# First cross attention: two heads scored in fp32 from the context, q stack turned on the chip, keys split in folded blocks, biases added on VectorE

## The reference

```python
q = heads(layernorm(x)); k = v = heads(ctx_1024)           # no projection here
u = einsum('hbqd,hbkd->hbqk', q, k) * scale / sqrt(16)
logits = tanh(u) * exp(log_C)
attn = softmax(where(mask, -inf, logits))
x = x + (attn @ v) @ W_out.T
```

## Time and profile before

| | us |
|---|---|
| median of 3 runs | 863.05 |
| lowest and highest | 860.47, 866.04 |
| profiled execution: span | 865.0 |
| TensorE busy in the span | 682.0 (79%) |
| ScalarE busy | 469.3 (54%) |
| VectorE busy | 432.3 (50%) |
| first cross attention, first score to last exp | 56.04 to 328.16 |

### The profile page before, as it was taken

The page is one execution under the profiler, slowest core; times in us unless marked ns, Lnnn a source line. Parts: engine busy times, 40 slices in busy tenths (PEclk is TensorE's granted clock), DMA queues, the critical chain, the costliest instruction groups (busy, mean ns, idle before and its releaser), DMA issues. The chain is left out here.

```text
span 865.0 us, 14147 instructions
## 1 busy us (share of the span) xinstructions
PE 682.0 (79%) x4916; PEld 375.2 (43%) x4916; DVE 432.3 (50%) x962; ACT 469.3 (54%) x554; POOL 64.0 (7%) x87
## 2 busy tenths in 40 slices
PE   0029789999999996495418999999999879957798
PEld 0013335544544543374203444444444456745686
DVE  6505422222232223765618887878778333644544
ACT  1236669999999995272003666656666605603010
POOL 6010001010010100000200000000000110000000
PEclk9999879999999998699556999999999969988799
DMA  7579843333333211000376222222221090000000
GB/s 231 137 211 296 221 134 106 100 106 92 117 100 102 89 36 49 0 1 1 85 145 199 69 68 68 66 68 68 66 74 58 18 311 1 2 1 0 1 1 12
DMA packets 55767, 75.93 MB, mean 88 GB/s; under 512 B 8756, under 2 KB 40886, under 8 KB 55734
## 3 DMA queue, kind: packets, MB, share of 16 engines
q1 hardware_dynamic: 50642, 72.87, 28.8%
q10 hardware_dynamic: 5092, 2.63, 1.2%
HBM read 61.06 MB, written 13.63 MB: 86 GB/s over the span
## 5 line engine op out<-in xcount | busy, mean ns | idle before, releaser
L1282 DVE TENSOR_REDUCE sb_m_blk<-ps 128x1 f32<-128x512 f32 x256 | 166.8, 687 | 56.0 <-PE ps L1180 55.4
L1143 ACT ACTIVATE sb_probs<-ps 128x1024 f32<-128x1024 f32 x128 | 129.4, 1023 | 62.4 <-PE ps L1207 62.0
L546 ACT ACTIVATE sb_probs<-ps 128x1024 f32<-128x1024 f32 x128 | 124.3, 1017 | 52.2 <-PE ps L571 49.2
L548 ACT ACTIVATE sb_probs<-sb_probs,sb_neg_cap,sb_cap 128x4096 f32<-128x4096 f32 x32 | 121.6, 3801 | 1.1
L1180 PE MATMUL ps<-sb_k_st,sb_q_m 96*128 96x512 bf16 x256 | 98.2, 405 | 27.3 <-issue 20.6
L571 PE MATMUL ps<-sb_q_st,sb_k_st 115*128 115x256 bf16 x512 | 77.9, 289 | 41.3 <-DMA sb_k_st<-k_parts_l 41.0
L1207 PE MATMUL ps<-sb_q_st,sb_k_st 115*128 115x256 bf16 x512 | 78.2, 275 | 9.7 <-ACT sb_q_st L1152 9.0
L571 PEld LDWEIGHTS ps<-sb_q_st,sb_k_st 115*128 115x128 bf16 x512 | 44.3, 102 | 94.2 <-issue 62.1
L584 PE MATMUL ps<-sb_probs,sb_v_st 128*32 128x256 f32 x1024 | 78.2, 403 | 3.8 <-ACT sb_probs L548 3.6
L1224 PE MATMUL ps<-sb_probs,sb_v_st 128*32 128x256 f32 x1024 | 78.5, 390 | 1.8
L1207 PEld LDWEIGHTS ps<-sb_q_st,sb_k_st 115*128 115x128 bf16 x512 | 48.8, 101 | 30.6 <-issue 11.8
(11 more groups left out here) (232 smaller groups left out, 867.9 us busy)
## 6 DMA issues: line engine op xcount, KB each, us to landing
sb_k_st<-k_parts_l SPq DMA_DIRECT2D x192, 128.0 KB, 2.7
k_parts_l<-sb_v_proj SPq DMA_DIRECT2D x24, 256.0 KB
k_parts_l<-sb_early SPq DMA_DIRECT2D x48, 128.0 KB
sb_k_st<-k_parts_l SPq DMA_DIRECT2D x64, 64.0 KB, 2.5
sb_early<-ctxT SPq DMA_DIRECT2D x8, 512.0 KB, 3.7
sb_probs<-ctxT SPq DMA_DIRECT2D x4, 512.0 KB, 7.5
sb_v_rows<-ctx ACTq DMA_DIRECT2D x1, 2048.0 KB, 16.4
sb_v_proj<-ctxT SPq DMA_DIRECT2D x4, 512.0 KB, 6.8
```

The lines of the kernel that those rows point to most:

```text
L546: a.activation(probs[:, j % 2, 4 * g:4 * g + 4, :], scores_bank(g), ACT.Tanh).then_inc(s["tanh"], 1)
L548: a.activation(probs[:, j % 2], probs[:, j % 2], ACT.Exp, bias=k.neg_cap[:, 0:1], scale=k.cap[:, 0:1]).then_inc(s["exp"], 1)
L1143: nc.scalar.activation(probs[:, g], scores_bank(g), ACT.Exp).then_inc(s["exp"], 1)
L1282: v.tensor_reduce(k.m_blk[:, q, blk:blk + 1], k.ps[:, 6 + idx % 2, :], AX.X, ALU.max).then_inc(s["m_read"], 1)
```

## The change

stage_prepare is gone and its work is inside stage_cross0. Heads 0 and 1 (the first four units) are scored in fp32: their channels of the transposed context are loaded straight into 16-row slabs at partitions 0, 32, 64 and 96 (`load_first_keys`), and each score group is four fp32 matmuls of 16 rows, two on each of two slabs (`qk_first`). The q stack is built from rows on VectorE (`split_rows`) and turned by 32 TensorE transposes (`turn`) instead of through DRAM. Both use the space of `k_st` until the loads for iteration 1. The split keys start at head 2, in seven blocks of 128 partitions x 1024 keys, where the first three fold two or four ranges of keys of the same heads onto the partitions. `kd0` is now laid out part, channel, key, and a unit's keys are read from it as 2 parts x 16 channels x 2048 keys for 32 destination rows. VectorE splits block 0 ahead of the first accumulator copy, and blocks 1 to 6 between the end of its first iteration and its second. The biases of the layer 1 projection are added on VectorE when the result is read, and the bias matmuls are gone. The early weights are loaded behind iteration 1, the context rows come in halves of keys on SyncE, and TensorE waits once for all expert weights.

```diff
-    k.kd0 = nc.dram_tensor("k_parts_l0", [H, PARTS * DH, S2], BF16, kind="Internal").ap()
+    k.kd0 = nc.dram_tensor("k_parts_l0", [PARTS, D, S2], BF16, kind="Internal").ap()
...
+    k.q_rows = k.k_st[:, 0:2, :]...
+    k.k_first = k.k_st[:, 2:4, :]...
...
-def store_k_parts(k, sp, n, parts):
...
+def load_first_keys(k, sp, e, units, done):
+
+    for r in range(2):
+        rows = slice(64 * e + 32 * r, 64 * e + 32 * r + DH)
+        src = k.i["ctxT"][e * DH:(e + 1) * DH, :].rearrange("d (u g r n) -> r d u g n", u=2, g=GROUPS, r=2)[r]
+        for u in units:
+            sp.dma_start(k.k_first[rows, u], src[:, u]).then_inc(done, 16)
+
+BLOCKS = [(2, 4, 0), (4, 2, 0), (4, 2, 1)] + [(8, 1, n) for n in range(SPLITS)]
...
+def store_block(k, sp, n, parts):
+
+    h0, folds, _ = BLOCKS[n]
+    rows = P // folds
+    sp.wait_ge(k.sem("k0_split"), n + 1)
+    for a in range(folds):
+        sp.dma_start(k.kd0.rearrange("s r n -> r s n")[h0 * DH:h0 * DH + rows, :, block_keys(n, a)],
+                     parts[a * rows:(a + 1) * rows, n % 2]).then_inc(k.sem(f"k0_stored{n % 2}"), 16)
...
+def load_k0_unit(k, sp, h, half, slot, loaded):
+
+    ks = slice(half * UNIT_KEYS, (half + 1) * UNIT_KEYS)
+    kd = k.kd0.rearrange("s (h d) n -> s h d n", d=DH)
+    for r in range(PARTS):
+        sp.dma_start(k.k_st[2 * DH * r:2 * DH * (r + 1), slot, :], kd[0:2, h, :, ks]).then_inc(loaded, 16)
+    sp.dma_start(k.k_st[LOROW:STACK, slot, :], kd[2, h, :, ks]).then_inc(loaded, 16)
...
-def stage_prepare(k):
...
@@ SP of stage_cross0
+            load_first_keys(k, sp, 0, [0], first_in[0])
+            load_ctx_rows(k, sp, 0)
+            load_first_keys(k, sp, 0, [1], first_in[1])
+            load_first_keys(k, sp, 1, [0, 1], first_in[2])
+            load_ctx_rows(k, sp, 1)
+            load_block(k, sp, 0, blk)
...
+            store_block(k, sp, 0, parts)
+            load_block(k, sp, 3, blk)
+            sp.wait_ge(k.sem("k0_stored0"), blocks_stored(0))
+            sp.wait_ge(s["q_turned"], H // 4)
+            for j in range(2):
+                load_keys(0, j)
+            for j in range(2):
+                store_kd1(0, j)
+            sp.wait_ge(s["scores"], 16)
+            for j in range(2, 4):
+                load_keys(0, j)
+            next_ctx(0)
+            for n in range(1, len(BLOCKS)):
+                store_block(k, sp, n, parts)
+                if 3 < n + 3 < len(BLOCKS):
+                    load_block(k, sp, n + 3, blk)
+            for n in (len(BLOCKS) - 2, len(BLOCKS) - 1):
+                sp.wait_ge(k.sem(f"k0_stored{n % 2}"), blocks_stored(n))
+            body(1, True)
+            load_early_weights(k, sp)
...
@@ POOL
-            link(g.memset(k.k_st[MAXROW:LOROW, :, :], 1.0))
-            link(g.memset(k.q_all[MAXROW:LOROW, :, :], 0.0))
...
@@ PE
+            def qk_first(j, g):
...
+                for c in range(2):
+                    for r in range(2):
+                        rows = slice(64 * e + 32 * r, 64 * e + 32 * r + DH)
+                        last = t.matmul(out[:, 2 * r + c, :], k.k_first[rows, u, g, c * P:(c + 1) * P], k.q_first[rows, :],
+                                        start=True, stop=True)
...
+            def turn(n):
...
+                        last = t.transpose(turned(n)[:, (h * QT + q) * P:(h * QT + q + 1) * P],
+                                           k.q_rows[:, q, 4 * n + h, :], k.ident_bf[:, :])
...
-                    last = t.matmul(o, k.bkv1[0:1, 0, j * P:(j + 1) * P], k.ones_row[0:1, 0:CBLK], start=False, stop=True)
...
-                        last = t.matmul(o, k.ones_row[0:1, 0:P], k.bkv1[0:1, 1, :], start=False, stop=True)
...
@@ DVE
-                v.tensor_copy(k.kd_bf[:, j, 0, :], src).then_inc(s["kd_ops"], 1)
+                v.tensor_scalar(k.kd_bf[:, j, 0, :], src, bias, None, ALU.add).then_inc(s["kd_ops"], 1)
...
+            split_rows(k, link, k.xn[:, :, :], k.q_rows).then_inc(s["q_rows"], 1)
+            for n in range(H // 4):
+                dve.wait_ge(s["q_turned"], n + 1)
+                v.tensor_copy(k.q_all[0:STACK, 4 * n:4 * n + 4, :].rearrange("p h q -> p (h q)"), turned(n)).then_inc(s["q_stack"], 1)
+            v.memset(k.k_st[MAXROW:LOROW, 0:2, :], 1.0).then_inc(s["k_ones"], 1)
+            split_block(0)
+            copy_acc(0, 0)
+            split_k(0, 0, True)
+            split_k(0, 1, True)
+            normalise(0, 0)
...
+            v_rows(0, 2)
+            v_rows(0, 3)
+            for n in range(1, len(BLOCKS)):
+                split_block(n)
+            body(1)
...
@@ last stage
-                pe.wait_ge(k.sem(f"f_exp_in{n}"), 48)
+                if n == 0:
+                    pe.wait_ge(k.sem("f_exp_in"), 16 * 3 * (N_EXP + 1))
```

More of the change, by code:

```diff
@@ L245, in layer_norm @@
     rsqrt(k, link, QT)
+def layer_norm(k, dve, link, src, dst, done):
+    v = k.nc.vector
+    norm_stats(k, link, src)
     for t in range(QT):
@@ L346, in load_early_weights @@
                      i["L0_attn_w_projT"].rearrange("(g m d) n -> m d g n", m=4, d=DH)[m]).then_inc(w2, 16)
-def stage_prepare(k):
[L351 to L384, removed]
-            link(g.memset(k.k_st[MAXROW:LOROW, :, :], 1.0))
-            link(g.memset(k.q_all[MAXROW:LOROW, :, :], 0.0))
[L389 to L440, removed]
-            dve.wait_ge(k.sem("pool_order"), 6)
-            for b in range(2):
-                link(v.tensor_copy(k.v_st[:, b, :, DH], k.keep[:, :]))
-        @block.tensor
-        def _(pe):
-            pe.wait_ge(k.sem("pool_order"), 2)
-            pe.wait_ge(k.sem("xn0"), QT)
-            transpose_rows(k, k.xn, 0, k.sem("xnT_ps"))
@@ L579, in pv @@
                     pe.wait_ge(s["exp"], 4 * it + j + 1)
-                    if j % 2 == 0 and not first:
+                    if first:
+                        if j == 0:
+                            pe.wait_ge(s["keep"], 3)
+                        pe.wait_ge(s["v_half"], (1, 3, 3, 4)[j])
+                    elif j % 2 == 0:
                         pe.wait_ge(s["o_read"], 2 * it + b - 1)
@@ L626, in body @@
                             if not (first and j == 0):
-                                pv(pit, pj, c, first)
+                                pv(pit, pj, c, fresh if j == 0 else first)
+                        if first and j == 1 and g == 0:
+                            turn(0)
+                            turn(1)
+                    if j == 1 and first:
+                        turn(2)
+                        turn(3)
                     if j == 1 and not first:
@@ L631, in body @@
                         sel(2 * it, 0)
-                    project(it, j, first)
-            pe.wait_ge(k.sem("w1_in"), 64)
+                    if not first:
+                        project(it, j, False)
+                    elif j >= 2:
+                        project(0, 2 * (j - 2), True)
+                        project(0, 2 * (j - 2) + 1, True)
+            pe.wait_ge(k.sem("pool_order"), 2)
+            pe.wait_ge(s["xq"], QT)
+            for q in range(QT):
+                last = t.transpose(k.ps[:, 7, q * P:(q + 1) * P], k.xq[:, q, :], k.ident[:, :])
+            last.then_inc(s["xqT"], 1)
             body(0, True)
-            with pe.Fori(1, H // 2) as it:
+            body(1, False, True)
+            with pe.Fori(2, H // 2) as it:
                 body(it, False)
@@ L712, in _ @@
+            for n in (len(BLOCKS) - 2, len(BLOCKS) - 1):
+                dve.wait_ge(k.sem(f"k0_stored{n % 2}"), blocks_stored(n))
+            with dve.Fori(2, H // 2) as it:
+                body(it)
             copy_acc(H - 1, 1)
```

273 lines of the change are left out of this document (187 added, 86 removed).

## The result

| | before | after |
|---|---|---|
| median (runs) | 864.54 (4) | 934.16 (4) |
| lowest to highest | 860.47 to 866.08 | 933.66 to 934.57 |
| ratio, 95% interval | | 1.081, 1.077 to 1.084 |
| profiled span | 865.0 | 932.9 |
| mean TensorE clock, share of 2.4 GHz | 0.919 | 0.864 |

The first score comes 45 us earlier, the last exp 63 us later, and the rest of the program loses 5 us more. ScalarE's timeline of the kernel after (start, length, line, tiles, count, and in brackets the idle time ahead with what ended it) shows both; it answers to the earlier trace rows.

A forecast was written before the change was run, and what follows sets the result against it. ScalarE bounds the first cross attention before, the two-engine key-load queue after. Stretches to 144.2, weights' iteration to 188.0, four iterations of 40.5 to 350.0, end 380.6: 52.4 us later, span 917.4, median 916, range 888 to 970.

The forecast's parts named there:

- The head: Start of the first cross attention: first scores at about 10.7 instead of 56.04, 45 us earlier.
- rival 3: First four units: fp32 units take twice as long, so the earlier start gives nothing; 12 us more, no separate chance.
- Two engines: Key loads read as 2x16x2048 are carried by two DMA engines: 7.87 us a unit, and the queue becomes the bound.
- The period: Steady cross attention iteration: 40.5 us, bounds 36.7 and 41.3, against 30.7 on ScalarE.
- gaps in the queue of 1 to 2 us at three places: Per iteration, the late context block and slow TensorE clock delay key loads, leaving the DMA queue empty.
- The sum: Cross attention's terms added up: stage end at 380.6 against 328.16, 52.4 later; span 917.4, median 916.
- then the keys of units 8 to 11 and a context block: 144.2: After the last block store lands at 107.5, the queue loads these until 144.2.
- The bound from below: Whole kernel on two engines with no gaps and a start 4 us better: 895.
- rival 2: Key loads on two slower engines, 19.1 GB/s each: iterations about 50 us, 121 later, 984; chance 0.16.
- Priced at nothing: Removed bias matmuls (22.2 + 19.8 us of TensorE), VectorE's sums and the one expert-weight wait: no effect on time.
- Rival 1: Key loads use all 16 engines after all: stage ends at 286.7, 41.5 earlier, 822; chance 0.12.
- key loads landing 10 us and more: Sign in the changed trace for two engines: key loads land this long after issue instead of 2.7.

The follow-up runs named there:

- e3: The kernel before with only the new kd0 layout, its 128x1024 stores and 2x16x2048 key loads: 969.64, ratio 1.121.
- e1: The changed kernel with each 32-row key load issued as two of 16 rows, seven transfers a unit instead of four: 842.41, ratio 0.973.
- e2: The changed kernel with stack rows ordered channel, part, so key loads read 16x2x2048 with the channel outermost: 839.90, ratio 0.970.
- e5: The changed kernel with the next context block issued on ScalarE's queue instead of SyncE's behind four key loads: 899.99, ratio 1.041.
- e8: The changed kernel with the early weights issued behind the loop, in the last iteration, which loads no keys: 923.83, ratio 1.066.
- e10: e9 with each projection of values computed twice from the second iteration on, the first pass overwritten: 831.51, ratio 0.962.
- e9: e2 with four of VectorE's block splits interleaved in its second body and the context block issued ahead of the third key load: 829.80, ratio 0.957.

## Why the prediction was right, point by point

The forecast was 916 and slower; it was slower, by 18 us more than forecast.

**The head held.** First tanh 12.26 against "near 11". VectorE's first small step behind the statistics took 0.17 where it had been 6.41, and q stood at 10.00; no run took GpSimd's clearings away by themselves. Groups of four fp32 scores follow each other by 1.71 us at first, the 1.72 of "the pair side by side" at the low level. Two groups in a row took 3.78 us at 32.67 and 2.00 at 49.68, so 1.0 each at the high level; rival 3 is out. The low level is read from durations here (sixteen value matmul records took 1.93 us at 22.88 and 1.07 at 51.61): the column of the granted clock says 1.00 from the start of the trace, in before too, and doesn't show it. Unit 4 began at 60.61 and not at 57; nothing followed from that, as unit 5 waited for the context anyway.

**Two engines held.** A share of 0.23 at 77 GB/s was forecast as "near 0.2 with some 75 to 80". e3 shows that the layout alone does it, e1 and e2 that 16 rows outermost undo it, with the same bytes in the same place of DRAM. The Trainium skill's rule (DMA: Bandwidth & Descriptors, "Why a DMA increments its semaphore by 16 and not by 1") gives 2 engines for after and 16 for e1 and e2. The traces agree with it: 0.13 at 53 GB/s in after with key loads under way, 0.80 in e2, and 0.37 over a whole stretch in both e1 and e2.

**The period held.** 40.5 was taken, 40.3 to 40.8 measured; e5, without the blocked context, gave 36.3 to 37.2, so the split into 36.7 of queue and some 4 that the context adds held. That these 4 are empty queue, "gaps in the queue of 1 to 2 us at three places", is seen at one place only: in windows of half a microsecond from 204 to 246 the share falls to 0.00 to 0.09 between 207.5 and 209.0, and else stays at 0.08 or more. Where the rest goes is open. The weights' 7.1 measured 6.7 (e8).

**What was short.** The sum ended the stage at 380.6, and it ended at 391.27. The step that failed is "then the keys of units 8 to 11 and a context block: 144.2": TensorE had that block at 153.79, 9.6 us later. Of these 3.8 are the start (the first load was issued at 111.29, not 107.5; VectorE was done at 107.4 and not 104). The other 5.8 are the stretch itself, 42.5 us from first issue to landing, for which I took 36.7, the bound without gaps, although I used 40.5 for the steady iterations. The same term was short once before: from 47.12 TensorE had the first such block at 88.34, 41.2 us later and not 36.7, and the forecast 83.7 was 4.6 too early. VectorE's wait for the block store behind it ended at 90.29 and not at 88, which is most of the late start. The trace shows SyncE held in issuing there:

```profile
111.29 2.05 SPq L408 DMA_DIRECT2D sb_k_st<-k_parts_l  x3
...
124.62 5.26 SPq L408 DMA_DIRECT2D sb_k_st<-k_parts_l  x3
...
136.84 0.43 SPq L467 DMA_DIRECT2D sb_early<-ctxT  x1
```

Little of the 5.8 is empty queue. In windows of half a microsecond the share is 0.00 until 112.5 and from 113.5 to 153.5 never under 0.11, so at most some 2 us are spent before the first bytes move. The rest passes with transfers under way: the usual window there has 0.12 at 49 GB/s, 24.5 for each of two engines where I took 25.5, and that makes 1.3 us of it. What slows the remainder stays open. From 153.79 to the last context block at 362.53 there are 208.7 us against 205.8, since the weights' iteration took 47.4 against 43.8: the gaps were left out of that one too. The end, 28.7 us against 30.6, gave 1.9 back.

So the stage has 10.7 of the 18 us, and the stretch behind it 4.8. The last 2.7 are the step from span to median: I took the median 1.4 below the span (863.05 is 2 below 865.0), and it stands 1.3 above it (934.16 and 932.9). The bound from below is 897 by its own terms, not 895. That 934 still lies inside the range is due to its width towards rival 2, not to these terms.

**Priced at nothing, wrongly.** That the bias matmuls run under ScalarE's 98% was true for their 42 us, but the stretch behind the stage grew by 4.8. This was a cover in the other direction, from work that seemed free to remove. On sixteen engines e10 took back 2.9 of e9's 3.8 by filling TensorE. In after, the same rows stand at 2.43 and 3.78 us; that it is the same cause there is argued from the rows alone, and e3 and e5 (below) show that the bias matmuls alone don't decide it.

**Rival 1** was priced at 822, and e2, which is that case, has 839.90. The stage ends at 296.76 instead of 286.7 because unit 6 starts at 96.97 and not 87, behind VectorE, and the stretch behind it takes 4.7 more; the rest is the step from span to median. So the change's idea was sound: with sixteen engines it saves 3%, with the two edits of order 4.3%. What was given back, some 94 us between e2 and after, is the layout.

**A sign that did not work:** "key loads landing 10 us and more". The page's median for them is 2.6, against 2.7 before, because it mixes both cross attentions. The context block's 14.4 against e2's 3.7 is the row that told.

## What to carry to other kernels

Before a DRAM tensor is laid out anew, write down the outermost dimension of each load and store that touches it: the same bytes made an iteration of 40.4 us on two engines and hid under one of 30.7 on sixteen. A transfer that gates an in-order engine should not be issued behind a long queue of others, nor behind a wait for another engine; here the first alone was worth 34 us (e5). And hidden work on TensorE may still matter to the clock of what follows: look at the first matmuls after the stage before calling its removal free.

## What the runs showed that I had not expected

- Issuing slows when two engines carry the queue: three key loads take SyncE 1.8 to 3.1 us in e2, and up to 7.58 us (at 186.16) in after; six kd1 stores took 4.00 us in e2 and 11.03 in after (52.30). One small bias load behind the context block and two weights took 5.63, against 0.45 in e2.
- The e5 kernel lost nothing behind the stage (536.5), though its bias matmuls are gone too: its last products took 1.93 and its output projection 2.93. The idle time ahead of the last products is the same 2.01 there. e3 is the other way round: bias matmuls kept, 0.56 us idle, and an output projection of 3.64. So neither this idle stretch nor the bias matmuls alone decide when the clock falls; what else does stays open.
- fp32 matmuls of 16 rows on two row slabs do run side by side, as the forecast had it: eight of 256 columns took 2.00 us at 49.68, about 0.5 us for each pair.
